# Attention and expert kernel on one core: scatter sends placed between selections, value blocks together, projection last, some selections on VectorE

## What is computed

```python
x = query                                   # 16 batches x 256 tokens x 128
xn = layernorm(x)
# attention: 16 heads of 8, causal
q, k, v = split(xn @ in_proj.T);  q = q / sqrt(8)
a = softmax(q @ k.T + causal_mask);  attn = (a @ v) @ out_proj.T
# experts: one shared, seven routed, top 2 of softmax(xn @ wr.T + rb)
ffn = expert_shared(xn) + sum_e w[e] * expert_e(xn)   # silu(h@g.T)*(h@u.T) @ d.T, 352 wide
out = x + attn + ffn
```

## Time and profile before

| | us |
|---|---|
| median of 3 runs | 509.91 (509.83 to 512.62) |
| the profiled execution, its own time | 512.13 |
| its span in the trace | 510.1 |

### The profile page before, as it was taken

The page is one execution under the profiler, slowest core; times in us unless marked ns, Lnnn a source line. Parts: engine busy times, 40 slices in busy tenths (PEclk is TensorE's granted clock), DMA queues, the critical chain, the costliest instruction groups (busy, mean ns, idle before and its releaser), DMA issues.

```text
span 510.1 us, 12198 instructions
## 1 busy us (share of the span) xinstructions
PE 458.3 (90%) x3919; PEld 328.0 (64%) x3923; DVE 350.2 (69%) x722; ACT 306.4 (60%) x661; POOL 296.1 (58%) x424
## 2 busy tenths in 40 slices
PE   8888998989878887878898999989899999979996
PEld 4766555646555554555565667868668788858874
DVE  6796998868766565665555048757667687656897
ACT  2756776757665565665555667646547676546653
POOL 1445997968767567667677540255364497856300
PEclk9999999979998699898756699999999999989999
DMA  9786999897753454355237024767767668730762
GB/s 249 234 256 216 317 317 308 289 377 252 249 158 110 124 147 153 96 159 152 89 106 273 22 86 141 228 207 226 242 210 247 223 195 279 246 119 28 227 196 72
DMA packets 60412, 99.80 MB, mean 196 GB/s; under 512 B 11045, under 2 KB 29226, under 8 KB 59328
## 3 DMA queue, kind: packets, MB, share of 16 engines
q1 hardware_dynamic: 55872, 90.57, 56.0%
q0 software_dynamic: 4480, 8.47, 4.9%
HBM read 60.85 MB, written 38.94 MB: 196 GB/s over the span
## 4 chain that ended last, share of the span: by engine, by line
PE 65%; ACT 8%; issue 5%; SPq 5%; another core or an unknown queue 5%; DVE 4%; DMA 2%; ACTq 0%; DVEq 0%; POOL 0%
PE ps L894 11%; PE ps L892 11%; PE ps L893 10%; PE ps L1042 6%; PE ps L975 6%; PE ps L983 5%; ACT sb_work L767 3%; PE ps L1046 3%; PE ps L1025 2%; PE ps L1210 2%; SPq L494 2%; PE ps L971 2%; PE ps L1027 2%; DMA sb_ring<-qk 2%
## 5 line engine op out<-in xcount | busy, mean ns | idle before, releaser
L1416 DVE TENSOR_REDUCE sb_blockmax<-ps 128x6 f32<-128x768 f32 x128 | 121.3, 955 | 67.2 <-PE ps L983 61.9
L767 ACT ACTIVATE sb_work<-ps 128x768 f32<-128x768 f32 x128 | 104.0, 813 | 79.2 <-PE ps L971 60.8
L663 POOL DMA_INDIRECT ys<-sb_v_all,sb_xn_all x76 | 79.3, 1043 | 76.0 <-DVE sb_v_all L1543 57.1
L635 POOL TENSOR_SCALAR_AFFINE_SELECT sb_work<-sb_work 128x512 f32<-128x512 f32 x128 | 82.2, 643 | 56.1 <-ACT sb_work L767 54.7
L893 PE MATMUL ps<-sb_ring,sb_wb 128*128 128x512 f32 (+5 forms) x231 | 83.2, 360 | 0.0
L975 PE MATMUL ps<-sb_ring 32*128 32x256 f32 x256 | 53.0, 406 | 29.4 <-ACT sb_work L767 23.2
L1521 DVE TENSOR_TENSOR sb_v_all<-ps,sb_v_all 128x512 f32<-128x512 f32 (+3 forms) x93 | 57.2, 615 | 25.7 <-ACT sb_v_all L839 10.4
L613 POOL DMA_INDIRECT xs<-sb_xn_all,sb_posu x64 | 62.2, 972 | 13.7 <-issue 13.7
L975 PEld LDWEIGHTS ps<-sb_ring 32*128 32x128 f32 x256 | 26.5, 196 | 60.3 <-issue 52.1
L983 PE MATMUL ps<-sb_mask_b,sb_ident_b 128*128 128x256 bf16 x256 | 55.1, 301 | 0.0
L839 ACT ACTIVATE sb_v_all<-ps 128x512 f32<-128x512 f32 (+3 forms) x93 | 49.5, 532 | 9.0 <-PE ps L894 5.4
(11 more groups left out here) (165 smaller groups left out, 1063.0 us busy)
## 6 DMA issues: line engine op xcount, KB each, us to landing
sb_wb<-wd SPq DMA_DIRECT2D x50, 384.0 KB
sb_ring<-qk SPq DMA_DIRECT2D x64, 256.0 KB
wd<-sb_wb SPq DMA_DIRECT2D x8, 1088.0 KB, 5.2
sb_wb<-wd SPq DMA_DIRECT2D x25, 320.0 KB
xs<-sb_o_all SPq DMA_DIRECT2D x19, 260.0 KB, 3.6
qk<-sb_ring SPq DMA_DIRECT2D x32, 128.0 KB
sb_work<-ys SPq DMA_DIRECT2D x16, 256.0 KB, 3.2
sb_xn_all<-xs SPq DMA_DIRECT2D x15, 260.0 KB
```

The lines of the kernel that those rows point to most:

```text
L635: pool.affine_select(out=o, in_=o, compare_op=ALU.is_ge, fill=0.0, base=0, pattern=[[0, 4], [1, 128]], channel_multiplier=-1)\
L663: pool.indirect_dma_start(out=ys_d, out_offset=bass.IndirectOffsetOnAxis(ap=row, axis=0), in_=yst[i % NYS][:, EMB * j:EMB * j + EMB], in_o ...
L767: act.activation(part.rearrange("p (k h q) -> p h k q", h=2, q=128), ps[:, 4:6, 0:HEAD].rearrange("p h (k q) -> p h k q", q=128), ACT.Exp, ...
L1416: dve.tensor_reduce(blockmax[:, p % 2, q, a:b + 1, 0:3], ps[:, a:b + 1, 0:HEAD].rearrange("p h (k c) -> p h k c", c=128), AX.X, ALU.max).t ...
```

## The change

Four edits, of which the first three concern how the streams are ordered:

1. GpSimd: sends no longer stand at the end of a step. In an even step one of the two comes ahead of the second selection and one behind it. In an odd step all of the step's sends (one or two) come between the two selections.
2. TensorE, `n >= 0`: in even steps both value blocks stand together ahead of the second half's scores, and `project(n)` is the last thing of the step.
3. For that, ScalarE copies the high part, and VectorE takes the low part, one step later, in the odd step (for `n < 0` nothing changes).
4. In the 20 even steps from 24 to 62 (`N_KEEP`) VectorE makes the first selection, as a minimum of the exponentials with a constant that is 3.4e38 on and under the causal line and 0 beyond it. This constant adds 128 columns to `const`. TensorE waits for a new semaphore `kept` beside `sel`.

```diff
-C_ALL = C_DEC + ROUTED
+C_KEEP = C_DEC + ROUTED
+C_ALL = C_KEEP + 128
+    c[:, C_KEEP:C_KEEP + 128] = np.where(p[:, None] <= p[None, :], 3.4e38, 0.0)
+        N_KEEP = range(N_SEND + 1, NQ, 2)
+        def selected(n):
+            return 2 * n + 2 - len([k for k in N_KEEP if k <= n])
@@ gpsimd
+                between = max(sent(n - 1), sent(n) - (n % 2 == 0))
                 if isq(n):
-                    for k in range(2):
+                    for k in range(n in N_KEEP, 2):
                         pair = PAIRS[1 - k]
+                        if k:
+                            sends(sent(n - 1), between)
                         pool.wait_ge(s["ex"], 2 * n + k + 1)
...
-                sends(sent(n - 1), sent(n))
+                sends(between, sent(n))
@@ scalar, step(n)
-                        if k and projected(n) is not None:
-                            projection_high(n)
+                        if k and n and projected(n - 1) is not None:
+                            projection_high(n - 1)
@@ tensor, value_sums
-                    pe.wait_ge(s["sel"], 2 * n + 2)
+                    pe.wait_ge(s["sel"], selected(n))
+                    if n in N_KEEP:
+                        pe.wait_ge(s["kept"], N_KEEP.index(n) + 1)
@@ tensor, step(n)
-                if projected(n) is not None:
+                if n < 0 and projected(n) is not None:
                     project(n)
                 if isq(n - 1):
                     value_sums(n - 1, 0)
-                    if projected(n) is None:
-                        value_sums(n - 1, 1)
+                    value_sums(n - 1, 1)
                 if isq(n) or isq(n + AHEAD):
                     scores(n, 1)
-                if isq(n - 1) and projected(n) is not None:
-                    value_sums(n - 1, 1)
                 if 0 < n < NQ + 2 and n % 2:
                     across(n)
                 if n >= 0 and isq(n + 2):
                     maxima(n + 2)
+                if n >= 0 and projected(n) is not None:
+                    project(n)
@@ vector, step(n)
-                if n >= 0 and projected(n) is not None:
-                    projection_low(n)
+                if n > 0 and projected(n - 1) is not None:
+                    projection_low(n - 1)
...
+                if n in N_KEEP:
+                    dve.wait_ge(s["ex"], 2 * n + 1)
+                    o = P[n % 2][:, HEAD * PAIRS[1][0]:HEAD * PAIRS[1][0] + 512].rearrange("p (k q) -> p k q", q=128)
+                    dve.tensor_tensor(o, o, const[:, C_KEEP:C_KEEP + 128].unsqueeze(1).to_broadcast([128, 4, 128]),
+                                      ALU.min).then_inc(s["kept"], 1)
```

More of the change, by code:

```diff
@@ L365, in build @@
         s_std = sem("s_std")
-        names = ("pq pk hq hk lq lk S max0 max1 mhi mx Mt q4b ST ex sel PV OT T xc rc nm busy "
+        names = ("pq pk hq hk lq lk S max0 max1 mhi mx Mt q4b ST ex sel kept PV OT T xc rc nm busy "
                  "xn xa nb xp xT xh xl V va lg tT oT wcp wsp rs var0 var rt rx selb id0 id1 cnts cnt pos tabs "
```

## The result

| | before, us | after, us |
|---|---|---|
| median on the chip of this comparison | 511.26 (4 runs, 509.83 to 514.72) | 495.1 (4 runs, 493.5 to 499.3) |
| ratio after / before | | 0.9687, 95% interval 0.9606 to 0.9768 |
| span of the profiled execution | 510.1 | 493.7 |

The change made this kernel 16.2 us faster here; 493 had been predicted, with a range of 480 to 507.

A forecast was written before the change was run, and what follows sets the result against it. No engine is full: a loop of waits bounds steps 24 to 62, with TensorE's signals held beside close sends. There 130.1 + 6.4 + 2.5 + 5 = 144.0 against 162.7; gain 18.7 - 1.6 = 17.1, so 493 us, range 480 to 507.

The forecast's parts named there:

- two close sends hold TensorE's signal: Steps 24 to 62: a close pair of sends delays the odd step's second exponential, costing 1.33 us a pair.
- the mean clock of the stage: Sign for the stage with sends: mean granted clock over 0.95, where it was 0.83.
- even step, first half: Steps 24 to 62: with TensorE's order that of an odd step, this half takes 1.45 us.
- even step, second half: Steps 24 to 62: block 1 (0.36) goes out of 1.60 us, the projection (0.52) comes in: 1.76 us.
- late selection and held signals, a pair: Odd step's second GpSimd selection 0.25 us late; signals held by single sends 0.3 us a pair, bounds 0 and 1.33.
- steps 0 to 23: Shorter even steps -2.2, late VectorE +1.5, later stores and reads +1.6; with first loads and first send +1.6 us.
- A single send costs a pair 0 or some tenths: Parted sends cost nothing unless a signal falls due in the hold; 0.3 us a pair taken.
- The four odd steps with two sends: Steps 31, 39, 47, 55: one more send between selections, 1.27 us all late, two still close; 4 x 1.6 = 6.4 us.
- The clock term: Steps 24 to 62: of 12.2 us beyond pairs at full clock, 5 us kept, bounds 0 and 12.
- the rival's up to 0.64 us for a meeting: VectorE's minimum meets a GpSimd selection; one waits up to 0.64 us, 20 times, 0.4 showing: +8, 501 us; 6%.
- Waits of `across` for the low part: Odd steps: TensorE's `across` waits for VectorE's low part when the division delays it; 0.25 us in ten pairs, 2.5 us.
- late reads of queries and keys: Rival: SyncE's stores wait for the low part, so reads behind come up to 1.6 us late per block: 501 us; 11%.

The follow-up runs named there:

- the half stand-in: Kernel before, second send of even steps 24 to 42 replaced by a GpSimd memset, both sends kept in 44 to 60: 490.71 us against 511.60 (chip E).
- the change with memsets: Kernel after with 60 of its 64 sends replaced by GpSimd memsets: 464.43 us against 476.27 for the kernel after (chip C).
- the four with single edits: Kernel before (512.65 us, chip B) with edit 1: 491.4; edits 2 and 3: 514.25; edits 1 to 3: 493.16; edits 1 and 4: 490.3.
- with the last four pairs spread too: Kernel before with edit 1, and the two sends of steps 31, 39, 47, 55 parted: 465.0 us on C (ratio 1.003), 466.62 on D (1.007).

## Why the prediction came out right, and where it didn't

**The time and the mechanism.** The time was 2 us off. The step on which all rests, that two close sends hold TensorE's signal in the odd step and parted ones hardly do, is shown by the half stand-in and by edit 1 alone. That the late first selection isn't what costs is shown too. In two ways the number was also lucky: the comparison ran where signals are held (beside 464.67 us on chip C the same change is slower), and terms that were wrong in opposite directions cancelled, as the table shows. One sign that was named didn't come: the mean clock of the stage is 0.91, not over 0.95.

**The terms for steps 24 to 62**, forecast against the trace of after:

| term | forecast | measured |
|---|---|---|
| even step, first half (before lateness and held signals) | 1.45 | 2.15 with both |
| even step, second half | 1.76 | 1.45 |
| odd step, first and second half | 1.45 + 1.46 | 1.69 + 1.45 |
| late selection and held signals, a pair | 0.25 + 0.3 | about 0.4 + 0.45, in the rows above |
| pair | 6.67 | 6.75 |
| all beyond 19.5 such pairs | 13.9 (6.4 + 2.5 + 5) | 146.0 - 131.6 = 14.4 |
| steps 24 to 62 | 144.0 | 146.0 (was 162.7) |
| steps 0 to 23 | +1.6, with the first loads and send | +1.8 (86.1, was 84.3) |

The pair came out right with two terms wrong in opposite directions. The second half wasn't 1.76: `project` at the end of the step lies in time in which the next exponentials run, and the half takes 1.45; the exponential at 142.44 shows no wait ahead of it, so this is ScalarE's own pace. Against that, the first half of the even step lost 0.70, not 0.25 plus a share of 0.3. The matmuls tell the two parts apart. Most even steps have them end 1.85 to 1.89 us after the first exponential; in steps 34, 42 and 58, where the selection isn't late, it is 1.45. So lateness costs about 0.4. The exponential then starts 0.28 to 0.41 us after their end in most even steps and 0.25 in the odd ones, where it is 0.03 to 0.06 in every step of the same kernel on chip C: that is the holding, 0.25 to 0.35 and 0.2. "A single send costs a pair 0 or some tenths" was right: it is about 0.45 for the three of them.

**What holds.** In the odd step of after, the send starts at 142.67, TensorE's last matmuls of the scores end at 143.88, and the exponential that needs only them starts at 144.13:
```profile
143.66 0.22 PE L982 MATMUL ps<-sb_ring 32*128 32x128 f32 x2
```
It starts 1.46 us after the send in this step and 1.55 after it in step 26 (139.44 to 140.99). Behind the second of two close sends it was 1.65 and 1.78 on chip E (199.23 to 201.01). A send thus seems to hold a signal that falls due in it to about 1.4 us after its start, a close second one somewhat longer, and above all two in a row leave no gap: the scores of an odd step fall due at the beginning of the second, and wait it out.

**The four odd steps with two sends** were mis-sized in their form, not in sum. Forecast were 6.4 us, and 5 for the clock in general. Measured, the four pairs cost 39.1 - 4 x 6.75 = 12.1 us, and three of the four have a low clock in them. The clock term wasn't general: it stands behind these steps, where TensorE pauses for the late selection, and in the pair of steps 60 and 61. That pair takes 8.7 to 9.5 us at a clock of 0.50 to 0.69 in every trace, before and after, so the change has no part in it. The chain of after at step 32 has the pause that was forecast (1.27 + 0.25 and a little):
```profile
159.50 1.60 issue
```

**VectorE.** The minimum takes 0.68 us; 0.65 was forecast. Lines of VectorE, 129 to 274 us:
```profile
L1467 DVE TENSOR_TENSOR sb_work<-sb_work,sb_const 128x512 f32<-128x512 f32 x19 | 12.9, 680 | 0.0
```
It had no wait of its own. The Trainium skill's rule (SBUF — State Buffer, "Who interferes with whom") had no occasion in the kernel after: in step 26 the minimum ended at 1.87 us after the first exponential and GpSimd's selection began at 3.14. In the change with memsets the two do meet, three times:
```profile
148.88 0.68 DVE L1485 TENSOR_TENSOR sb_work<-sb_work,sb_const 128x512 f32<-128x512 f32 x1
149.27 0.78 POOL L664 TENSOR_SCALAR_AFFINE_SELECT sb_work<-sb_work 128x512 f32<-128x512 f32 x1 [1.41 <-ACT sb_work L796]
```
They overlap for 0.29 us. The minimum, which came first, keeps its 0.68, and the selection takes 0.78 where 0.63 is usual. The order agrees with the rule, but 0.15 us is less than a full block of 0.29 would cost, so the rival's up to 0.64 us for a meeting was set high, as far as this overlap tells. Waits of `across` for the low part come to at most 1.8 us in the stage, for 2.5 forecast.

**Steps 0 to 23.** The forecast of late reads of queries and keys can be seen in the chain of after, beside the earlier trace rows, where one such read of 7.93 us stood:
```profile
57.14 8.09 DMA sb_ring<-qk
...
101.06 8.66 DMA sb_ring<-qk
```
But the +1.8 itself isn't shown. The same 24 steps took 84.3 and 85.5 us in two traces of before and from 83.7 to 88.0 in the four with single edits, without order by edit.

**What failed.** Two steps of the argument. First, worth was put on edits 2 to 4: the even half was to become shorter. With real sends they give nothing (491.4 with edit 1 alone, 493.16 with 1 to 3, ratios that overlap), and where nothing is held the whole change loses 3%. The prediction named the late second selection but not that the projection in its old place covered part of it, nor that VectorE's selection would move a send under TensorE's signal. Second, all rivals took for granted that the holding, read from one trace, belongs to the kernel. It doesn't belong to the kernel alone: the same program has it on A and not on D. Whether the chip makes the difference or something else that differed between the sessions isn't shown, since no chip was used twice. A trace of one chip could not have told that. But a rival "there is no hold to remove, and the four late selections still cost their 6.4 us and some clock" could have been sized with the prediction's own terms, and it ends at slower.

**Still open.** Why signals are held on A, B and E and not on C and D. Whether it is GpSimd's issuing of the indirect DMA or the traffic that follows which holds them: the memset has neither. Also why the rest of the program, which has indirect DMAs too, is longer on the first kind: from the first exponential of step 63 to the end 218.1 us in the trace that was predicted from (the earlier trace rows and the span) and 202.7 on D, for the same kernel before. All 14 traces fall into these two groups, 216.6 to 218.1 us on A, B and E and 202.4 to 203.0 on C and D. Whether that is the same cause was not tried.

## What to carry to other kernels

Where one engine issues indirect DMAs beside a loop of semaphores, look at who gets a signal during them and how long after the work's end: the matmuls' end against the start of what waits for them, in two timelines. Don't put two such issues together, and don't put two ahead of work that a third engine waits for. Parting the sends (edit 1) gained 4.4% where signals are held; with the last four pairs spread too, it cost at most 0.7% where they aren't. Before paying for that with moved work on other engines, test the one edit alone, and on more than one chip.

## What the runs showed of the hardware that wasn't expected

- The kernel before takes 511 to 513 us on chips A, B and E and 463 to 465 us on C and D, 10% apart. Within steps 24 to 62 this is 162.7 against 131.3 us. What differs in the traces there is when TensorE's signals take effect beside GpSimd's sends, 1.65 us after the matmuls' end (chip E) or 0.05 (chip D), and the granted clock, 0.83 or 0.98.
- With a memset of 0.97 us on GpSimd in the place of a second send of 0.96, the exponential of the odd steps starts 0.04 to 0.23 us after the matmuls' end, not 1.38 to 1.82 (chip E, full clock).
- Sending the same 64 scatters in another order makes 4.4% on one kind of chip (edit 1: 0.956) and less than 1% on the other (1.003 and 1.007, with the four pairs spread too).
- A pause of TensorE of 1.27 us behind a late selection was followed by a granted clock of 0.72 over 12 us, where the 28 us before it had 1.00. What a late wait costs is thus more than its length: in the kernel after the four such pairs cost 12.1 us for pauses of 1.60 to 1.64 us.
